# Correction matmuls of a perceiver layer on two row tiles, and one transpose of Q moved ahead on VectorE

## What is computed

```python
x = x + xattn(layernorm(x), ctx_4096)     # both rounded to 8 bits, then one matmul with ctx (2, 2048, 2048)
x = x + attn(layernorm(x), Wq, Wkv, Wo)   # 32 heads of 64 over one shared K and V, ALiBi, causal
x = x + ffn(layernorm(x), qweight, qzeros, scales, bias)
# ffn: W[i, o] = scales[g(i), o] * (nibble[i, o] - (zero[g(i), o] + 1)), 16 groups of 128 rows; x @ W + bias
```

## Time and profile before

| | us |
|---|---|
| median of 3 runs | 394.89 (394.87 to 394.91) |
| the profiled execution, its own time | 394.95 |
| its span | 393.1 |

### The profile page before, as it was taken

The page is one execution under the profiler, slowest core; times in us unless marked ns, Lnnn a source line. Parts: engine busy times, 40 slices in busy tenths (PEclk is TensorE's granted clock), DMA queues, the critical chain, the costliest instruction groups (busy, mean ns, idle before and its releaser), DMA issues.

```text
span 393.1 us, 5711 instructions
## 1 busy us (share of the span) xinstructions
PE 348.2 (89%) x2342; PEld 264.6 (67%) x2342; DVE 325.4 (83%) x322; ACT 223.5 (57%) x320; POOL 29.7 (8%) x69
## 2 busy tenths in 40 slices
PE   0076765799999998999999999999999999999995
PEld 0021231425888887888888888888888788888884
DVE  1779989796878499975999949989997999999923
ACT  1788988998615983844875661652844933333000
POOL 6000000005591000000010000000000000000000
PEclk9999989899999999999999999999999999999999
DMA  8999999999155487396639716695000020000006
GB/s 328 425 436 430 424 428 428 427 401 394 46 197 163 176 198 233 110 219 210 213 111 278 238 65 203 227 333 201 2 1 1 2 107 2 0 0 2 0 0 213
DMA packets 21958, 77.37 MB, mean 197 GB/s; under 512 B 1354, under 2 KB 1402, under 8 KB 18810
## 3 DMA queue, kind: packets, MB, share of 16 engines
q1 hardware_dynamic: 21924, 77.01, 54.2%
q10 hardware_dynamic: 8, 0.00, 0.0%
HBM read 74.91 MB, written 2.10 MB: 196 GB/s over the span
## 4 chain that ended last, share of the span: by engine, by line
PE 72%; DMA 13%; ACT 6%; DVE 5%; issue 3%; ACTq 0%; DVEq 0%
PE bank L1189 22%; PE bank L1052 13%; PE bank L1053 13%; PE bank L1054 13%; DMA raw<-in_ctx 12%; ACT q L463 4%; PE bank L1065 2%; PE bank L1135 2%; PE bank L1153 2%; DMA prm_row<-in_L_xattn_x_zp 2%; PE bank L1045 1%; PE bank L1075 1%; DVE stats L625 1%; PE bank L1103 1%; DVE resid L723 1%
## 5 line engine op out<-in xcount | busy, mean ns | idle before, releaser
L487 ACT ACTIVATE w_hi<-raw 128x2048 fp32r<-128x2048 f32 x29 | 55.3, 1912 | 45.0 <-DMA raw<-in_L_attn_Wq 23.4
L655 DVE TENSOR_TENSOR w_lo<-raw,w_hi 128x2048 fp32r<-128x2048 f32 x27 | 62.1, 2315 | 11.0 <-ACT w_hi L487 11.0
L1189 PE MATMUL bank<-w_hi,hd 128*128 128x512 f32 x208 | 53.1, 391 | 0.1
L1013 PE MATMUL bank<-q,at 128*128 128x512 bf16 x128 | 35.8, 405 | 17.6 <-DVE q L711 17.0
L1189 PEld LDWEIGHTS bank<-w_hi,hd 128*128 128x128 f32 x208 | 38.8, 188 | 8.4 <-issue 0.5
L711 DVE TENSOR_SCALAR q<-q 128x2048 bf16<-128x2048 uint8 x32 | 38.4, 1218 | 3.5 <-PE bank L1020 2.2
L1052 PE MATMUL bank<-w_hi,hd 128*128 128x512 f32 x104 | 40.6, 390 | 0.0
L1053 PE MATMUL bank<-w_lo,hd 128*128 128x512 f32 x104 | 40.5, 389 | 0.0
L1054 PE MATMUL bank<-w_hi,hd 128*128 128x512 f32 x104 | 40.5, 389 | 0.0
L1052 PE MATMUL bank<-w_hi,xt 128*128 128x512 f32 x96 | 38.2, 397 | 0.0
L1053 PE MATMUL bank<-w_lo,xt 128*128 128x512 f32 x96 | 37.4, 390 | 0.0
(11 more groups left out here) (160 smaller groups left out, 611.5 us busy)
## 6 DMA issues: line engine op xcount, KB each, us to landing
raw<-in_ctx SPq DMA_DIRECT2D x8, 2048.0 KB, 15.1
raw<-in_L_attn_Wq SPq DMA_DIRECT2D x16, 1024.0 KB, 6.2
ctx_more<-in_ctx SPq DMA_DIRECT2D x7, 2048.0 KB, 15.7
raw<-in_L_attn_Wo SPq DMA_DIRECT2D x13, 1024.0 KB, 5.2
raw_fifth<-in_L_attn_Wo SPq DMA_DIRECT2D x3, 1024.0 KB, 5.1
resid<-in_x SPq DMA_DIRECT2D x2, 1024.0 KB, 12.6
ctx_more<-in_ctx SPq DMA_DIRECT2D x2, 1024.0 KB, 15.3
scale<-in_L_ffn_scales SPq DMA_DIRECT2D x16, 128.0 KB, 6.5
```

The lines of the kernel that those rows point to most:

```text
L487: nc.scalar.activation(hi_slots[s], raw_slots[s], ACT.Copy).then_inc(w_hi_set, 1)
L655: nc.vector.tensor_tensor(lo_slots[s], raw_slots[s], hi_slots[s].bitcast(F32), ALU.subtract).then_inc(w_lo_set, 1)
L1013: mm(bank[:, 4 * b + n, :], at[:, k, b * P:(b + 1) * P], q16[:, i % 2, n * CH:(n + 1) * CH], start=start, stop=False)
L1189: return mm(bank[:, 4 * b + n, :], left[:, j, b * P:(b + 1) * P], right[slot_of(W_F + j)][:, n * CH:(n + 1) * CH], start=part == 0 and j = ...
```

## The change

Two things are changed. `corr` and `group_sum` get a new layout: the 128 rows are two halves of 64, the first batch's in the lower and the second batch's in the upper, and each half holds its three blocks at offsets 0, 16 and 33 with the bias at 32 and 49. `correction()` now issues for each chunk of columns one matmul on rows 0 to 63 for the first batch and one on rows 64 to 127 for the second, in alternation. This takes 12 loads of scales and zeros in place of 6, and 4 of the bias in place of 2; `part_lo` is made on DVE early in the context stage by `lower_rows()`, from sums over columns of the identity matrix. And in the attention loop of DVE `q_blocks(2n)` stands before `heads_lo(n-1)`.

```diff
+HALF = P // 2
+CORR_AT = (0, 16, 33)
+BIAS_AT = (32, 49)
...
                 if w == W_O + RING:
                     sp.wait_ge(corr_zero, 1)
-                    for blk in range(3):
-                        r = slice(CBLK * blk, CBLK * blk + GROUPS)
+                    for at in [HALF * b + s for b in range(B) for s in CORR_AT]:
+                        r = slice(at, at + GROUPS)
                         sp.dma_start(zraw[r, :], qzeros).then_inc(corr_loaded, 16)
                         sp.dma_start(corr[r, :], scales).then_inc(corr_loaded, 16)
             sp.wait_ge(corr_set, 1)
-            for blk in range(2):
-                sp.dma_start(corr[CBLK * blk + GROUPS:CBLK * blk + GROUPS + 1, :],
-                             bias.unsqueeze(0)).then_inc(bias_loaded, 16)
+            for at in [HALF * b + s for b in range(B) for s in BIAS_AT]:
+                sp.dma_start(corr[at:at + 1, :], bias.unsqueeze(0)).then_inc(bias_loaded, 16)
...
+            def lower_rows():
+                dve.wait_ge(idents_set, 4)
+                dve.wait_ge(masks_set, 1)
+                halves = ident[:].rearrange("p (b c) -> p b c", b=B)
+                for x, (start, stop) in enumerate(((CORR_AT[1], CORR_AT[2]), (CORR_AT[2], BIAS_AT[1]))):
+                    link(nc.vector.tensor_reduce(part_sum[:, x, :], halves[:, :, start:stop], AXX, ALU.add))
+                    nc.vector.scalar_tensor_tensor(out=part_lo[:, x:x + 1], in0=part_sum[:, x, 0:1], scalar=-1.0,
+                                                   in1=part_sum[:, x, 1:2], op0=ALU.mult,
+                                                   op1=ALU.subtract).then_inc(part_set, 1)
...
             selector()
+            lower_rows()
             convert_ctx(2)
...
+                if n < NCH:
+                    q_blocks(2 * n)
                 heads_lo(n - 1)
                 if n < NCH:
-                    q_blocks(2 * n)
                     q_blocks(2 * n + 1)
...
             def correction():
-                for b in range(B):
-                    for n in range(NCH):
-                        mm(bank[:, 4 * b + n, :], rsum[:, b * P:(b + 1) * P], corr_r[:, n * CH:(n + 1) * CH],
+                for n in range(NCH):
+                    for b in range(B):
+                        rows = slice(b * P // 2, (b + 1) * P // 2)
+                        mm(bank[:, 4 * b + n, :], rsum[rows, b * P:(b + 1) * P], corr_r[rows, n * CH:(n + 1) * CH],
                            start=False, stop=False)
```

More of the change, by code:

```diff
@@ L41 @@
 NPAIR = KT // 2
-CBLK = 32
+HALF = P // 2
+CORR_AT = (0, 16, 33)
+BIAS_AT = (32, 49)
 W_Q, W_O, W_F, W_END = 0, 16, 32, 48
@@ L153, in perceiver @@
         part_lo = sb("part_lo", [P, 2], F32)
+        part_sum = sb("part_sum", [P, 2, B], F32)
         row_no = sb("row_no", [P, 1], I32)
@@ L248, in perceiver @@
         corr_zero = sem("corr_zero")
+        part_set = sem("part_set")
         corr_set = sem("corr_set")
@@ L295, in sum_copies @@
         def sum_copies(b):
-            return group_sum[:, b, CBLK:3 * CBLK].rearrange("p (k c) -> p k c", k=2)[:, :, 0:GROUPS]
+            at = HALF * b + CORR_AT[1]
+            return group_sum[:, b, at:at + 2 * (GROUPS + 1)].rearrange("p (k c) -> p k c", k=2)[:, :, 0:GROUPS]
         def sums_twice(b):
-            return group_sum[:, b, 0:GROUPS].unsqueeze(1).to_broadcast([P, 2, GROUPS])
+            return group_sum[:, b, HALF * b:HALF * b + GROUPS].unsqueeze(1).to_broadcast([P, 2, GROUPS])
         def slot_free(engine, w):
@@ L414, in _ @@
             link(nc.gpsimd.memset(group_sum[:], 0.0))
[L415 to L420, removed]
+            for b in range(B):
+                for s in BIAS_AT:
+                    link(nc.gpsimd.memset(group_sum[:, b, HALF * b + s:HALF * b + s + 1], 1.0))
+            nc.gpsimd.memset(part_sum[:], 0.0).then_inc(masks_set, 1)
             pool.wait_ge(masks_set, 1)
@@ L578, in _ @@
                 upper_w(w)
-            act.wait_ge(bias_loaded, 16 * 2)
+            act.wait_ge(bias_loaded, 16 * 4)
             attention_over(act)
@@ L587, in group_sums @@
                     rows = work[:, b, g * GROUPSIZE:(g + 1) * GROUPSIZE]
-                    ins = nc.scalar.activation(rows, rows, ACT.Copy, accum_out=group_sum[:, b, g:g + 1])
+                    ins = nc.scalar.activation(rows, rows, ACT.Copy, accum_out=group_sum[:, b, HALF * b + g:HALF * b + g + 1])
                 if g == GROUPS - 1:
@@ L928, in _ @@
             remainder_w(W_O + 7)
-            dve.wait_ge(corr_loaded, 16 * 6)
-            rows = slice(0, 3 * CBLK)
+            dve.wait_ge(corr_loaded, 16 * 12)
+            rows = slice(0, P)
             zi = corr_z[rows, :].bitcast(I32)
@@ L947, in _ @@
             dve.wait_ge(corr_hi, 1)
+            dve.wait_ge(part_set, 2)
             nc.vector.scalar_tensor_tensor(out=corr_r[:], in0=corr_up.bitcast(F32), scalar=part_lo[:, 0:1],
```

## The result

| | before | changed |
|---|---|---|
| median, us | 394.99 (394.87 to 395.39, 10 executions) | 393.88 (393.77 to 394.01, 10 executions) |
| the profiled execution, us | 394.95 | 393.88 |
| its span, us | 393.1 | 392.1 |

The ratio is 0.9965, 95% interval [0.995, 0.998]: a small gain of 0.3%, 1.1 us at the median, clear of the noise. The forecast was 393.66, with 393.3 to 394.6 as its range.

A forecast was written before the change was run, and what follows sets the result against it. PE was taken to bound the kernel from 155 us on. The profiled 394.95 less 0.60 (transpose) and 0.63 (correction) gives 393.72; the median lies 0.06 below, so 393.66, range 393.3 to 394.6.

The forecast's parts named there:

- What bounds the kernel: From 155 us on PE is the bound, busy 231.64 of 231.75 us; work it saves comes off the end.
- The transpose, 0.60: Hole before the second scores: one transpose of Q moved into DVE's idle time starts PE 0.60 us earlier.
- My doubt: DVE's unexplained 0.47 us before the heads' lower part might meet any first instruction, leaving only 0.1 to 0.2 saved.
- The rival in which only the correction gains: The 0.47 us on DVE eats the transpose's gain: 394.1 to 394.2; chance 0.13, shared with part of each gain.
- The correction, 0.63: Correction's eight matmuls on PE: pairs side by side take 0.93 + 0.3 = 1.23 in place of 1.86, saving 0.63 us.
- the change of shape: PE's change between whole array and row tiles at the correction, into tiles and back, put at 0.3 us together.
- Tiles in turn: Rival at the correction: each tile loads, then multiplies, losing 0.3; 394.6, down to 394.2; chance 0.13 for tiles without overlap.
- The four small instructions, 0.96, covered: Two reductions and two combinations on DVE near 27 us take 0.96 us, absorbed by slack in the context stage.
- The correction's loads: Six more loads on SP from 209.7 us: the Wo granule lands at 224.5, covered with 1.7 us left.
- The slower case of the rivals: Wo granule too late, PE waits near 230 us: 395.6, or 397.4 at 9 us of landing time; chance 0.05.
- The bias loads: Two more bias loads delay the granule behind them by 0.58 us, covered because PE multiplies it 19 us later.
- The size: Whole kernel: likeliest time 393.66 us, both gains as computed; chance 0.60 for 393.3 to 394.0.

The follow-up runs named there:

- e2_corr_only: Changed kernel with the transposes of Q back in their old places, so only the correction's part remains; median 394.22 us, ratio 0.9993.
- e3_both_ahead: Changed kernel with, in the first group, both transposes of Q ahead of the heads' lower part and one weight remainder behind it; 394.27 us, ratio 0.9979.
- e4: Changed kernel with the correction's four matmuls on rows 0 to 63 issued first, then the four on rows 64 to 127; 394.55 us, ratio 0.9984.
- e8: Changed kernel with both first-group transposes of Q ahead and the four small DVE instructions moved out of the context stage; 393.82 us, ratio 0.9969.
- e9: Changed kernel with all eight correction matmuls on rows 0 to 63, the second batch's half of the sums left out; 394.87 us, ratio 1.0001.
- e12: Changed kernel with a second load of the same row, into an unused buffer, behind each of the four bias loads; 393.98 us, ratio 0.9976.
- e5: Changed kernel with the four small DVE instructions moved from the context stage to before the first residual sum of Wo; 394.08 us, ratio 0.9981.
- e6: Changed kernel with the correction issued twice, 16 matmuls on row tiles in place of 8; 396.33 us, ratio 1.0032.
- e10_bias_behind: Changed kernel with granule W_O+12 issued ahead of the four bias rows on SP's queue; median 393.99 us, ratio 0.9973, one execution 398.3.

## Why the prediction was right, and where it wasn't

**What bounds the kernel.** Right. PE is full from the scores on, and what it gained at the hole and at the correction is the 1.07 us.

**The transpose, 0.60.** The profile shows 0.59, and the place, the order and the remaining hole (0.54, forecast 0.5 to 0.6; scores at 154.86, forecast 154.85) are as worked out. The step itself is only half shown. 0.60 is the second transpose's time, and it was counted from a start at 152.95 that held 0.37 us of a delay without a cause. `e2_corr_only` has the old order without it, and against that profile the move is worth 0.25. So the size came out in part by luck: the row that it was read from held the delay. What the delay was stays open. My doubt was that this delay would fall on whichever instruction came first and eat the gain; `e3_both_ahead` shows 0.10 for the hand-over. The rival in which only the correction gains, with 0.1 to 0.2 for the move, is out by the profiles. Its time, 394.1 to 394.2, is near the second median of the changed kernel (394.24), but there too the profiled execution has a hole of 0.54, so that time has another reason.

**The correction, 0.63.** It gained 0.53. The steps were right, 4 x 0.232, shown by doubling them. The mis-sized term is the change of shape, put at 0.3 and measured at 0.41: I had counted the way in, the first whole matmul behind and the last tile's end, and left out that the first pair takes 0.34 as well.

**Tiles in turn.** This rival didn't occur, and the rule under it isn't borne out: pairs overlap in either order, and on one tile the loads hide.

**The four small instructions, 0.96, covered.** 0.59 and covered. The nearest rows had been too long for them: 0.18 and 0.16 each, where I took 0.26 and 0.22.

**The correction's loads.** Forecast: the granule at 224.5, 1.7 us left. Measured: 222.82 and 2.8 left. The granule went out at 212.86, 0.49 later than before (forecast 0.1), and the stretch of slow transfers, 212 to 218, moved 144 to 151 GB/s, where I had taken the 120 of the six loads before. The slower case of the rivals, a wait of PE near 230, didn't occur in any profile.

**The bias loads.** This is the step that failed. It did no harm in the first ten executions. I took 0.58 us for two more rows, and seven half granules, 19 us, for the cover. SP's queue shows 0.93 more for them, and 19 us is when PE multiplies W_O+12 itself. But DVE stands in between: everything behind W_O+12 in its order shifts with it, and the last lower part of Wo has 1.8 us. The 0.93 fits in that; a landing 3.1 us late doesn't. Nor had I counted that a PE that comes 0.59 sooner takes that much from the 2.5 us that were there. The cover of a delay is the smallest along the whole chain behind it, not that of the instruction that meets it first.

**The size.** 393.66 against 393.88: 0.10 at the correction, 0.05 lost between the scores and it, 0.01 at the hole, and 0.06 since the median of these runs lay on the profiled execution and not below it. That it came so near is luck in part: the forecast held nothing for the long executions, of which the first ten had none. Where the changed kernel was run again, its median was 394.24, 0.58 above the forecast and still in its range.

## What to carry over

Where a small matmul can be cut in two halves of rows, two 64-row tiles run at once in any order, but going into tiles and back costs about two starts of a matmul, 0.4 us here: the eight gained 0.53 of 0.93. A load whose landing varies needs its slack counted down to the last consumer of the engine that works in order behind it; a bounding engine that gets faster takes from that slack. A granule whose slot is free shouldn't stand behind rows that wait for a result. And a step that doesn't need a weight shouldn't stand behind that weight's remainder.

## What was new about the hardware

- Two row tiles of 64 overlap even when four matmuls of one are issued before the first of the other: 1.13 us for eight in both orders.
- A change between whole array and tiles costs 0.41 us over four starts, 0.09 to 0.11 each.
- A 1 MB load at the same place, with the same work around it, was taken up 5.05 us after its issue in the changed kernel's two profiles, 5.1 to 5.9 in five others (e2, e3, e4, e8, e9), 5.5 behind doubled bias rows (e12), and 8.2 in e5 and e6.
- The granted clock fell from 1.00 to 0.50 (2.4 and 1.2 GHz) for some 3 to 7 us two or three times in the context stage, at places that changed from one profile to the next; the stage's end moved by no more than 0.45 us between all profiles.
- In `e10_bias_behind` the clock fell to 0.50 for some 3 us behind one idleness of 3.13 us in the stage where PE is the bound, and that cost 1.55 us besides the idleness.
